# Two fused transformer-like layers on one core: the first two iterations issued in one joint order, the last three reordered

## The reference, cut to what matters

```python
# layer 0: attention over 512 positions, 8 heads of 32, queries serve as keys and values
q      = x.T @ Wq.T
logits = (scale * q q^T * cmask + (1 - cmask) * -1e30) * rmask
x      = x + (softmax(logits) @ q @ Wo.T).T
# layer 1: attention over 256 rows, 16 heads of 32
ss     = cond @ W_emb + b_emb                    # scale and shift of each batch
xn     = rms_norm(x) * g_norm * (1 + scale) + shift
q,k,v  = split(xn @ W_qkv);  q,k = rms_norm per head
o      = softmax(q k^T / sqrt(32)) @ v
out    = x + o + o @ W_out
```

## Time and profile before

| | |
|---|---|
| times of three runs | 1313.63 us median, 1311.67 to 1318.56 |
| the profiled execution | 1316.98 us, of which the span of its instructions is 1315.2 |
| PE busy | 1247.5 us (95%) |
| DVE busy | 1034.5 us (79%) |
| POOL, ACT busy | 773.4 us, 767.3 us |
| mean granted PE clock | 0.969 of full |
| iteration 0 ends, iteration 1 ends (PE) | 104 us, 181 us |
| one iteration from 2 on | 75.6 us |
| iteration 15, PE | 1163.7 to 1243.1 us |
| iterations 16 and 17, PE | 1243.1 to 1312 us |

### The profile page before, as it was taken

The page is one execution under the profiler, slowest core; times in us unless marked ns, Lnnn a source line. Parts: engine busy times, 40 slices in busy tenths (PEclk is TensorE's granted clock), DMA queues, the critical chain, the costliest instruction groups (busy, mean ns, idle before and its releaser), DMA issues.

```text
span 1315.2 us, 20714 instructions
## 1 busy us (share of the span) xinstructions
PE 1247.5 (95%) x6768; PEld 581.5 (44%) x6768; DVE 1034.5 (79%) x916; ACT 767.3 (58%) x1393; POOL 773.4 (59%) x391
## 2 busy tenths in 40 slices
PE   6979899999999999999999999999999999998877
PEld 4424354544444454444445454444545444443433
DVE  4665778878887887889787888888788888877654
ACT  1525566665656666565657666566666656564514
POOL 0245658476665838575574847566583766647442
PEclk8769899999999999999999999999999999999998
DMA  8322544437253433636354342735444363632332
GB/s 279 98 52 78 113 105 99 108 84 169 82 142 101 112 98 92 150 81 162 94 117 111 91 119 81 170 89 124 110 102 107 91 161 82 147 77 57 83 68 61
DMA packets 77960, 143.01 MB, mean 109 GB/s; under 512 B 21536, under 2 KB 23072, under 8 KB 77856
## 3 DMA queue, kind: packets, MB, share of 16 engines
q1 hardware_dynamic: 69136, 126.17, 39.1%
q10 hardware_dynamic: 8720, 15.51, 3.9%
HBM read 32.02 MB, written 8.39 MB: 31 GB/s over the span
## 4 chain that ended last, share of the span: by engine, by line
PE 80%; POOL 6%; issue 4%; DVE 3%; ACT 3%; SPq 2%; ACTq 1%; DMA 1%; POOLq 0%; DVEq 0%
PE PX L530 25%; PE PS L442 9%; PE PO L469 8%; PE PX L564 7%; PE PS L456 6%; PE PO L491 5%; POOL RQK L1928 5%; PE PM L411 4%; PE PX L508 2%; PE PM L508 2%; PE PO L494 2%; PE PM L420 2%; SPq L2071 1%; PE PM L480 1%; PE PM L548 1%
## 5 line engine op out<-in xcount | busy, mean ns | idle before, releaser
L1040 ACT ACTIVATE E<-PS,KBIAS 128x512 f32<-128x512 f32 x512 | 340.0, 686 | 199.0 <-PE PS L442 151.3
L530 PE MATMUL PX<-WQKV,XNT 128*128 128x512 f32 x768 | 383.9, 603 | 3.1 <-ACT V L1018 1.6
L1539 DVE TENSOR_REDUCE NM<-PM 128x4 f32<-128x2048 f32 x128 | 292.1, 2282 | 79.4 <-PE PM L411 79.4
L1916 POOL TENSOR_TENSOR E<-E 128x1024 f32<-128x1024 f32 x112 | 263.1, 2368 | 120.8 <-PE PO L469 107.6
L442 PE MATMUL PS<-B,A 97*128 97x512 f32 x512 | 288.1, 600 | 6.2 <-ACT E L1040 5.3
L1946 POOL TENSOR_TENSOR KQLO<-E 128x1024 f32<-128x1024 f32 x64 | 151.5, 2368 | 229.3 <-ACT E L1047 227.6
L1928 POOL TENSOR_TENSOR RQK<-RQK,HALF 128x16 f32<-128x16 f32 x64 | 211.1, 3303 | 96.6 <-DVE RQK L1627 96.6
L1047 ACT ACTIVATE E<-PS 128x512 f32<-128x512 f32 x256 | 146.9, 597 | 111.1 <-PE PS L456 110.9
L530 PEld LDWEIGHTS PX<-WQKV,XNT 128*128 128x128 f32 x768 | 136.5, 190 | 103.7 <-issue 89.1
L1546 DVE TENSOR_REDUCE NM<-PM 128x8 f32<-128x2048 f32 x64 | 146.4, 2288 | 37.5 <-PE PM L420 37.4
L442 PEld LDWEIGHTS PS<-B,A 97*128 97x128 f32 x512 | 93.3, 192 | 161.6 <-issue 110.2
(11 more groups left out here) (80 smaller groups left out, 1354.3 us busy)
## 6 DMA issues: line engine op xcount, KB each, us to landing
A<-QHI SPq DMA_DIRECT2D x256, 64.0 KB, 2.0
B<-QHI SPq DMA_DIRECT2D x256, 64.0 KB, 2.0
A<-KQHI SPq DMA_DIRECT2D x128, 128.0 KB, 2.4
B<-KQHI SPq DMA_DIRECT2D x128, 128.0 KB, 2.4
XB<-x SPq DMA_DIRECT2D x16, 512.0 KB, 4.0
A<-QLO SPq DMA_DIRECT2D x128, 64.0 KB, 2.0
B<-QLO SPq DMA_DIRECT2D x128, 64.0 KB, 2.0
X<-x ACTq DMA_DIRECT2D x16, 512.0 KB, 4.9
```

Of the source, the lines that this page charges most:

```text
L530: last = mm(PX[:, :], XNT[:, c, t * P:(t + 1) * P], WQKV[:, c, part * DM:(part + 1) * DM], start=(c == 0), stop=(c == 3))
L1040: fn(E[:, probs(seg, i, g), h, :], PS[n % 2][:, :], ACT.Exp, bias=KBIAS[:, g, b:b + 1], scale=SCALE).then_inc(exp_done, 1)
L1539: v.tensor_reduce(NM0[:, q, :].rearrange("p (h k) -> p h k", k=KB0)[:, :, kb], PM[:, :, :], axis=AX.X, op=ALU.max, negate=True).then_inc(m ...
L1916: g_.tensor_tensor(running(seg, i)[:, heads_, :], running(seg, i)[:, heads_, :], E[:, probs(seg, i, g), heads_, :], ALU.add).then_inc(done, 1)
```

## The change

It leaves the function `iteration` and so iterations 2 to 14 as they are. What it does, part by part:

1. **Joint order.** `iteration_0` and iteration 1 become one list on each engine, `iterations_0_and_1`, in which the first eight scores of batch 1's half A, its `values0` and others stand ahead of, or between, the last steps of iteration 0. `project0` and the first quads of batch 1 stand earlier in iteration 0.
2. **Loads.** `WEMB` gets the place of `B1` instead of `E`. SP issues it right behind the first `x`; `WO`, `WQKV` and `WOUT` are issued by SP in iteration 0, after three of the four stacks of batch 1's half A and ahead of the fourth. ACT issues five small DMAs at once and waits for none. The modulation stands in two blocks of four, behind the third and the fourth quad.
3. **Two queues for stacks.** ACT issues four of batch 0's eight stacks, and one of batch 15's four in layer 1.
4. **Iteration 15** has new lists on all engines; on POOL the step `masked_out` stands behind the last `norm_heads`.
5. **Iteration 16.** The odd `qk` write PSUM bank 3 of `PM` instead of `PX`. `norm_heads` is DVE's there. The maxima are transposed and sent to row 97 in two halves, each with four DMAs on ACT. `keep_x1` stands ahead of the last exponential.
6. **Iteration 17** has its `out1` parts in another order.

A function `keep_warm` is added and never called.

```diff
-        WEMB = E[:, 0:2, :, :].rearrange("p a h t -> p (a h t)").rearrange("p (c n) -> p c n", c=4)
+        with nc.sbuf_tensor("WEMB", [P, 4, 2 * DM], F32) as WEMB:
+            pass
+        def heads_bank(b, k):
+            return PM[:, 3, :] if b == NB - 1 and k % 2 else PX[:, :]
+            def rows1_half(i, b, j):
+                pe.wait_ge(context_taken, CONTEXT_TAKEN.ahead(("n1", j), i))
+                pe.wait_ge(max_done, MAXES.upto(("c", 2 * j + 1), i, QUAD))
+                tp(PO[0:H1, j * P:(j + 1) * P], NM1[:, j * H1:(j + 1) * H1], IDENT[:, :]).then_inc(n1_half[j], 1)
...
             def loads():
-                act.wait_ge(wq_in.sem, 16)
-                act.wait_ge(xin_in.sem, xin_in.at(0))
                 act.dma_start(CT[:, :, :], cond_t).then_inc(ct_in.sem, 16)
...
+            def rows1_half(i, b, j):
+                act.wait_ge(n1_half[j], 1)
+                copy(NMT1[0:H1, j, :], PO[0:H1, j * P:(j + 1) * P]).then_inc(context_taken, 1)
+                for h in range(QH):
+                    act.dma_start(B1[96:97, h, 2 * j:2 * j + 2, :].rearrange("p c (k t) -> p (c k) t", t=P).bitcast(F32),
+                                  NMT1[h * QH:(h + 1) * QH, j, :].bitcast(F32)).then_inc(row1_half_in[j], 16)
...
             def iteration_16(i):           # ACT
...
+                stack1(i, i - 1, 3)
+                rows1_half(i, i - 1, 0)
                 values1(i, i - 1, 0)
...
             def iteration_before(i):       # SP
+                load_modulation()
+                load_x(i + 2)
                 stack0(i + 1, 0, 0)
...
+            def iterations_0_and_1(i):     # SP
+                load_mask(i)
+                stack0(i + 1, 0, 2)
+                stack0(i + 1, 0, 1)
+                stack0(i + 1, 0, 3)
+                load_weights()
+                stack0(i + 1, 0, 0)
```

More of the change, by code:

```diff
@@ L324, in cond_resid @@
         n1_full = ev("n1_full", 1)
+        n1_half = [sem(f"n1_half{j}") for j in range(2)]
+        row1_half_in = [sem(f"row1_half_in{j}") for j in range(2)]
         row1_in = ev("row1_in", 16)
@@ L382, in small, with modulation, keep_warm @@
                 return PM[:, k, :]
+            def modulation(*ns):
+                pe.wait_ge(mod_in.sem, 16 * 3)
+                pe.wait_ge(ct_in.sem, 16)
+                for n in ns:
+                    for c in range(4):
+                        last = mm(PO[:, n * NB:(n + 1) * NB], WEMB[:, c, n * P:(n + 1) * P], CT[:, c, :],
+                                  start=(c == 0), stop=(c == 3))
+                if ns[-1] == 7:
+                    last.then_inc(mod_full.sem, 1)
+            def keep_warm(n):
+                pe.wait_ge(ident_set.sem, 3)
+                for _ in range(n):
+                    mm(PS[1][:, 0:P], IDENT[:, :], IDENT[:, :], start=True, stop=True)
             def quad_free(key, i):
@@ L529, in project1 @@
                 for c in cs:
[L530 removed]
+                    last = mm(bank, XNT[:, c, t * P:(t + 1) * P], WQKV[:, c, part * DM:(part + 1) * DM],
                               start=(c == 0), stop=(c == 3))
```

849 lines of the change are left out of this document (576 added, 273 removed), and 12 rows, old and new, of the table special.

## The result

The changed kernel took 1305.04 us (median of 6 runs, 1299.12 to 1307.46) against 1316.2 us (median of 6, 1311.67 to 1318.56) for the kernel before on the same chip: a ratio of 0.9918, 95% interval 0.9899 to 0.9937. It is faster by 0.8%, where 1.1% was forecast, and the time lies inside the range. Its profiled execution took 1304.76 us, span 1302.5, against 1316.98 and 1315.2.

A forecast was written before the change was run, and what follows sets the result against it. PE bounds the steady iterations, chains between engines the two ends. Terms -0.5 + 0.5 - 5.5 - 7 - 2.5 = -15 took the profiled 1316.98 us to 1302.0; against the median 1313.63, 1298.6, rounded to 1299 us; range 1286 to 1309.

The forecast's parts named there:

- Start: Up to the row of maxima: a gain of 1.2 us, spent on batch 1's projection before the first score; -0.5 us.
- Iteration 0, half B: Batch 1's filling stands before the last weighted values, which end near 87.4; first layer 1 projection unchanged near 103.9; +0.5 us.
- the weights hold up batch 1: Rival, iteration 0: weights issued ahead of head 0's stack delay batch 1's scores and `out0`; 1321.6 us, chance 0.05.
- Iteration 1: 5.5 us of PE work moves into iteration 0's waits and DVE's chain allows it; -5.5 us, bounds nothing and -13.
- the filling is given back: Rival: DVE sets iteration 1's end, gaining only 1 us; iteration 15 gives 4, the end 1; 1307.6 us, chance 0.16.
- Iteration 15: Moving `masked_out` removes PE's 4.03 us wait and low-clock time; new lists give 1.5; -7 us, between -4 and -10.
- Iterations 16 and 17: The end: earlier stacks, two queues, row halves and `keep_x1` sum to -2.5 us, between +1 and -8; iteration 17 gives 0.
- Two queues: Iteration 16: one of four stacks issued by ACT, limited by shared DMA engines; -1.5 us, by issue time alone -3.9.
- Row DMAs on ACT: Iteration 16: the second half row costs ACT four issues between the third and fourth exponential; +1.3 us.
- `keep_x1` ahead of the last exponential: Iteration 16: this 1.05 us copy precedes the exponential that the final context waits for; +0.5 us net.
- The chains dissolve: Rival: iterations 0, 1, 15 and 16 become bound by PE alone, gains reach upper bounds; 1286 us, chance 0.2.
- the signs that I had named as wrong: Wait on `DMA A<-QHI` near 88; iteration 2 near 181 with DVE always busy; batch 15's third layer 1 score stack-held past 43 us.

The follow-up runs named there:

- w_early: Changed kernel with the three weight loads issued ahead of, not behind, three stacks of batch 1: 1297.5 us, ratio 0.9865 to the kernel before.
- before_mask: Kernel before with only POOL's `masked_out` of iteration 15 moved behind the last head product: 1314.22 us, ratio 0.9978 to the kernel before.
- The best: Changed kernel with early weight loads, modulation spread over PE's waits, second row half on SP, half A's transposed values earlier: 1295.23 us, ratio 0.9839.

## Why the prediction was right, and where it was not

The profiled pair differs by 12.7 us of span, where the sum gave 15. Every term but that of iteration 0 came within 0.6 us of its forecast; of their mechanisms, only that of iteration 15 came out whole. Step by step:

- **Start, -0.5 forecast.** The first score moved from 40.01 to 39.85. Right as far as it can be told, since the same start came 1.9 us sooner in w_early; the weights of the modulation were no wait.
- **Iteration 0, half B, +0.5 and an unchanged first layer 1 projection at 103.9.** This step failed. It came at 106.12, 2.2 us late. I let the last weighted values end at 87.4 us, by adding batch 1's filling to the durations of before. They ended at 81.40, and before at 86.92. Of these 5.5 us, the last exponentials ended 1.4 sooner; the sums and the values ran in 1.06 and 1.07 us instead of 1.94 each, 1.8; and the quad that stood between the two, with its wait of 1.00 us for DVE, stands earlier now, 1.7. Most of the rest is DVE's last addition (1.22 us instead of 2.07). From there the rival "the weights hold up batch 1" describes what happened: weights issued 72.4 to 74.1 (forecast 74), the stack usable at 89.09 (forecast 88.5). Its mechanism and its landing time were right, and I dismissed it by comparing the landing with an arrival of PE that was 6 us too late. (Its break-even of 147 GB/s leaves out the 2.5 us of the stack behind the weights, which the 130 GB/s and 111 us count in; with them it is 160 to 170.) With the loads moved (w_early), this stage, from the first score on, is 5.2 us shorter than before instead of 2.4 longer. I had taken that gain for none at all.
- **Iteration 1, -5.5.** The profiled pair gives -5.0, and the near match is luck. First, the eight transposes were no gain: before, they stood ahead of the first layer 1 projection already (lines 50 and 51 of the order before), so by my own prices 4.4 us of work left, not 5.5. Second, PE's idle time in the iteration rose from 5.65 to 7.63 us: the rival "the filling is given back" took 2.0. Third, the clock gave the rest: before, PE did 11.6 us of its work in iteration 1 at 0.50 (2.2 at the start, 9.4 in 147 to 157 us), in the changed kernel 1.3. PE's busy time fell by 7.0, which leaves about 2.6 to the clock (an estimate: 7.0 less 4.4). And 73.0 us is the shortest of the eight kernels with late weights and the changed iteration 1 (73.0 to 75.2, mean 74.4), while the two with the order of before took 78.0 and 77.3. By the means it is -3.3. Among the eight the idle time is the same (7.6 to 7.7 us), so their spread is clock. No run has the joint order without the moved loads, so what each of the two is worth stays open.
- **Iteration 15, -7.** Measured -6.7, and the mask alone gave -5.2 and, taken back, +5.5. Right, in its parts too: the mask has the wait of 4.03 and the low clock behind it, and the new lists have the 1.5 between before_mask and the changed kernel, as forecast.
- **Iterations 16 and 17, -2.5.** Measured -3.1, right by luck. The stacks start 3.7 us sooner (forecast 2.8), of which the products on DVE are 2.5. Two queues: -1.3 (forecast -1.5), but with a loss of 2.1 at the first score that I had not seen. Row DMAs on ACT: +0.6 at most (forecast +1.3). `keep_x1` ahead of the last exponential: -0.9, and I had +0.5: the collision that it prevents was no part of the term. These sizes are single executions, and against the other execution of the old tail the whole term is only -0.2; of waiting on PE it saved 1 to 2 us.

"The chains dissolve" did not come, and no version here reached its 1286, which moreover took 5 us for the tail where the upper bound was 8. The best took 1295.2, and what it gained over the changed kernel lies in iteration 0 and the start, for which that rival had nothing. Of the signs that I had named as wrong, one appeared, the wait for a stack near 88 (on `B<-QLO`), and one half: iteration 2 started at 179.1, between the 175.5 of right and the 181 of wrong. What stays open is how much of the medians' 11.2 us belongs to the tail, for which executions of the old tail differ by 2.9 us.

## What to carry to other kernels

When bulk loads share a queue with small transfers, put them where the queue is idle and where they land before the first small one is due, also a small one of another queue; the margin must be counted from the earliest time that the consumer could ask, at its full clock, and not from the time at which it asked before. An operation that waits for a load belongs behind what others wait for on its engine, however short it is. And before an operation is moved off the path at the tail, look whether it holds two others apart.

## What the runs showed of the chip

- The same matmuls at the same place ran at different speeds from one execution to the next. The second projection of the start, four matmuls at 10.45 us, took 3.75 us in the changed kernel and 1.95 in w_early at 10.48, with nothing different ahead of it (first projection at 5.83 and 5.86); the first score moved by 1.9 us with it. The profile gives a clock of 1.00 for both, so that this is the clock is inferred: four of the same matmuls took 1.96 us in iteration 1 at 1.00 and 3.78 at 68.44 us at 0.50. Such stretches cost 1.9 us at the start, 2.1 at the start of iteration 1 and 2.9 at the tail, as much as most single steps of this change.
- Behind a gap of 7.7 us in its work PE was granted 1.2 GHz for 8 us, and the first half of `out0` took 3.62 us where it takes 1.98 in iteration 1. But w_early, without that gap, had a low stretch of 3.4 us at the same place and needed 3.09, so the gap is not shown to be the only cause.
- A DMA of 8 KB on ACT's queue took 5.2 us to land while SP's weights kept the DMA engines at 1.03 of their time, and 1.8 us when they were idle.
- A DVE product with two inputs in SBUF, 0.4 us long, took 2.58 us when it met a POOL addition, while reciprocals that overlapped such additions for a part kept their 1.75 us.
